# The last step of a one-layer vision tower written out by hand, with the last five tiles gated together

## The reference, cut to what matters

```
h = patches @ tok_W                                        # 768 -> 256
x = layernorm(h)
mod = gelu(x @ w1 + b1) @ w2 + b2                          # 256 -> 1024 -> 256
m = (x @ in_w + in_b) * mod
y = irfft(rfft(m over an image's 196 tokens) * rfft(taps))
h = h + y @ out_w + out_b
x = layernorm(h)
gate = softmax(x @ router_W.T + router_b)                  # 6 experts, the best 2 kept
h = h + x @ base_W.T + base_b + shared(x)
      + sum over experts of gate_e * (x @ A_e.T) @ B_e.T   # rank 16
```

## Time and profile before

| | us |
|---|---|
| median of 3 runs | 1297.09 (1296.03 to 1297.81) |
| the profiled execution, its own time | 1294.84 |
| span of its trace | 1293.0 |
| TensorE busy | 1239.2 (96%) |
| VectorE busy | 868.5 (67%) |
| ScalarE busy | 585.6 (45%) |
| GpSimd busy | 399.8 (31%) |

### The profile page before, as it was taken

The page is one execution under the profiler, slowest core; times in us unless marked ns, Lnnn a source line. Parts: engine busy times, 40 slices in busy tenths (PEclk is TensorE's granted clock), DMA queues, the critical chain, the costliest instruction groups (busy, mean ns, idle before and its releaser), DMA issues.

```text
span 1293.0 us, 21070 instructions
## 1 busy us (share of the span) xinstructions
PE 1239.2 (96%) x8148; PEld 1199.4 (93%) x8148; DVE 868.5 (67%) x2584; ACT 585.6 (45%) x1108; POOL 399.8 (31%) x462
## 2 busy tenths in 40 slices
PE   5999999999999999999999999999999999999964
PEld 5999999999999999999999999999999999999953
DVE  6467666667766666766666776666677666677575
ACT  6644544444444445454444444443545444444410
POOL 4532333232233333233323223332323332322100
PEclk9999999999999999999999999999999999999986
DMA  7111111101111110111110111111011111010000
GB/s 236 37 38 50 49 50 38 49 13 50 49 50 50 37 39 24 50 49 50 37 50 13 50 49 50 50 37 46 18 50 49 50 37 50 15 48 13 13 1 33
DMA packets 23182, 57.18 MB, mean 44 GB/s; under 512 B 2665, under 2 KB 18218, under 8 KB 19114
## 3 DMA queue, kind: packets, MB, share of 16 engines
q1 hardware_dynamic: 22266, 55.05, 12.2%
q10 hardware_dynamic: 816, 0.79, 0.2%
HBM read 42.98 MB, written 12.85 MB: 43 GB/s over the span
## 4 chain that ended last, share of the span: by engine, by line
PE 90%; DVE 5%; ACT 2%; issue 1%; POOL 1%; DMA 0%; POOLq 0%; DVEq 0%
PE rotating L953 16%; PE rotating L955 16%; PE rotating L954 16%; PE rows_ps L953 10%; PE rows_ps L954 10%; PE rows_ps L955 10%; PE turn L1095 5%; PE turn L1079 2%; ACT x_h L449 2%; DVE x_l L702 2%; PE turn L992 2%; PE turn L953 1%; PE turn L954 1%; PE turn L955 1%; PE rotating L1060 1%
## 5 line engine op out<-in xcount | busy, mean ns | idle before, releaser
L471 ACT ACTIVATE gelu<-rotating,biases 128x392 f32<-128x392 f32 x256 | 149.0, 583 | 203.6 <-PE rotating L955 203.4
L382 POOL TENSOR_TENSOR folded<-modulated 128x196 f32<-128x196 f32 x64 | 38.5, 601 | 588.1 <-DVE modulated L793 588.1
L369 POOL TENSOR_TENSOR gelu_l<-gelu,gelu_h 128x784 fp32r<-128x784 f32 x62 | 117.1, 1889 | 225.8 <-DVE norm L776 199.8
L354 POOL TENSOR_TENSOR patches_l<-patches,patches_h 128x384 fp32r<-128x384 f32 x186 | 184.4, 1020 | 0.2 <-ACT patches_h L429 0.2
L953 PE MATMUL rotating<-gelu_h,w_h 128*128 128x392 f32 x512 | 177.6, 347 | 0.0
L953 PE MATMUL rotating<-x_h,w_h 128*128 128x392 f32 x512 | 177.1, 346 | 0.0
L953 PE MATMUL rows_ps<-tokw_h,patches_h 128*128 128x256 f32 x576 | 167.8, 291 | 7.5 <-POOL patches_l L360 7.5
L955 PE MATMUL rotating<-x_h,w_l 128*128 128x392 f32 x512 | 174.6, 341 | 0.0
L954 PE MATMUL rotating<-x_l,w_h 128*128 128x392 f32 x512 | 174.5, 341 | 0.0
L955 PE MATMUL rotating<-gelu_h,w_l 128*128 128x392 f32 x512 | 174.0, 340 | 0.0
L954 PE MATMUL rotating<-gelu_l,w_h 128*128 128x392 f32 x512 | 173.9, 340 | 0.0
(11 more groups left out here) (203 smaller groups left out, 3007.2 us busy)
## 6 DMA issues: line engine op xcount, KB each, us to landing
patches<-dram_x_rest SPq DMA_DIRECT2D x31, 1152.0 KB, 5.1
out<-h_sb SPq DMA_DIRECT2D x32, 384.0 KB, 2.5
patches<-dram_x_first SPq DMA_DIRECT2D x3, 384.0 KB, 4.9
h_sb<-dram_x_second SPq DMA_DIRECT2D x1, 768.0 KB, 8.3
prod<-dram_tok_w ACTq DMA_DIRECT2D x2, 256.0 KB, 5.4
gelu<-dram_w SPq DMA_DIRECT2D x1, 512.0 KB, 6.4
norm<-dram_w SPq DMA_DIRECT2D x1, 384.0 KB, 6.1
gelu<-dram_w SPq DMA_DIRECT2D x1, 384.0 KB, 7.0
```

Source lines behind the costliest of these rows:

```text
L354: pool.tensor_tensor(patches_l[:, k, :], patches[:, k, :], patches_h[:, k, :].bitcast(F32), ALU.subtract).then_inc(pool_patches_lo, 1)
L369: pool.tensor_tensor(gelu_l[:, 2 * j:2 * j + 2, :], gelu[:, 2 * j:2 * j + 2, :], gelu_h[:, 2 * j:2 * j + 2, :].bitcast(F32), ALU.subtract)\
L471: act.activation(gelu[:, k, :], bank(g + 1, UP[k])[:, 0:GT], ACT.Gelu, bias=b1_bias[:, k:k + 1]).then_inc(act_gelu, 1)
```

## The change

The loop over i ends at 31. Step 32 and all that follows it stand in an order of their own, for each engine. In short, as against the order before (`last` is 31):

- In step 32 TensorE does the first two of eight parts of `mlp_down(31, 0)` ahead of `inverse_dft(30)` and the rest behind it, and `mixer_tiles(30)` stands after the first two parts of `mlp_down(31, 1)`. DVE does `gelu_lo(31, 2)` ahead of `spectrum_of_y(30)` and `finish(29)` after `gelu_lo(31, 3)`. `modulate(31, 0)` stands right after `y_lo(30)`, and `modulate(31, 1)` inside the chain of the layer norm (`meanwhile`). Before, both stood behind the chain and the normalisation.
- `turn_x2(30)` stands behind `turn_fold(31)`; `dft(31)` ahead of `base_route(30)`.
- `gate_exp(30)` moves from between `spectrum_of_y` and `whole_y` to after `normalise(31)`; `gate(30)` from there to after `x2_lo(32)`; `routed(30)` from ahead of `turn_x2(31)` to after the base products of the last tiles. Round 32 is normalised by ACT (`last_normalise`) while DVE does round 31.
- The five tiles of rounds 31 and 32 get one gate of 25 + 1 instructions. TensorE first makes only the 102 routing columns for all five (30 products, `last_routes_products`), and their 256 base columns later (30 products, `last_base_products`). The five tiles' scratch space and two constants, loaded by SP in step 31 ahead of the store of round 28, lie in the free buffer `patches`.
- The last output goes in three parts (two tiles, one, two), each added and stored once its products are done. POOL writes two rows of constants for it.

```diff
+LAST_TILES = 5
+LAST_PLACES = ((0, 0), (0, 1), (1, 0), (2, 0), (2, 1))
+LAST_BANKS = ((0, 1), (2,), (3, 4))
...
+        last_base = (rotating[:, 0], rotating[:, 1], turn[:, 0])
+        last_routes = turn[:, 1, 0:LAST_TILES * ROUTE_COLS].rearrange("p (t c) -> p t c", t=LAST_TILES)
+        last_gated_h, last_gated_l = y_h[0:ROUTED + 1, 0, :], y_l[0:ROUTED + 1, 0, :]
...
 @block.sync
-            for i in range(1, GROUPS + 1):
+            for i in range(1, GROUPS):
                 if i + 2 < ROUNDS:
                     load_patches(i + 2)
+                else:
+                    sp.wait_ge(pool_patches_lo, KT * (ROUNDS - 2))
+                    sp.dma_start(last_thr, last_rank_thr_d).then_inc(last_consts, 16)
+                    sp.dma_start(last_bias, last_router_bias_d).then_inc(last_consts, 16)
...
 @block.gpsimd
+            last = GROUPS - 1
+            pool.wait_ge(gate_done, last - 1)
+            gelu_lo(last, 0)
+            gelu_lo(last, 1)
+            fold(last, 0)
+            fold(last, 1)
+            pool.wait_ge(pe_out, 2 * last + 3)
+            pool.memset(y_h[ROUTED:ROUTED + 1, 0, :].bitcast(F32), 1.0).then_inc(last_ones_row, 1)
+            pool.memset(y_l[ROUTED:ROUTED + 1, 0, :].bitcast(F32), 0.0).then_inc(last_ones_row, 1)
...
 @block.scalar
+            y_sine(last - 1)
+            y_hi(last - 1)
             fold_hi(last)
+            x2_hi(last - 1, rows_ps, x2_h)
             y_sine(last)
             y_hi(last)
-            gated_hi(last - 1, turn[:, 0])
+            last_normalise()
             x2_hi(last, turn, x2_h)
             x2_hi(last + 1, rotating, x1_h)
-            gated_hi(last, rotating[:, 2])
-            gated_hi(last + 1, rotating[:, 2])
+            gated_hi(last - 1, rotating[:, 2])
+            last_gated_hi()
...
 @block.vector
+            fold_lo(last - 1)
+            gate_exp(last - 2, round_routes, round_room)
+            gate(last - 2, round_routes, round_room)
+            real_products(last - 1)
+            gated_lo(last - 2, bank(GROUPS, TURN_GATED))
+            imaginary_products(last - 1)
+            gelu_lo(last, 2)
+            spectrum_of_y(last - 1)
+            gelu_lo(last, 3)
+            finish(last - 2, rows_ps)
+            whole_y(last - 1)
+            y_lo(last - 1)
+            dve.wait_ge(dve_y_lo, DH * last)
+            modulate(last, 0)
+            add_mixer(last - 1, rows_ps[:, 2], bank(GROUPS, OUT)[:, 0:DIM])
+            stats = stats2(last - 1, 1)
+            layer_norm_scales(GROUPS + 1, stats, slice(1, 2), 3, meanwhile=lambda: modulate(last, 1))
+            normalise(last - 1, norm2, 1)
             fold_lo(last)
+            x2_lo(last - 1, rows_ps, x2_h, x2_l)
             real_products(last)
             imaginary_products(last)
             spectrum_of_y(last)
-            gate_exp(last - 1, rows_ps)
             whole_y(last)
             y_lo(last)
-            gate(last - 1, rows_ps)
             add_mixer(last, rotating[:, 1], rotating[:, 2, 0:DIM])
...
             normalise(last, norm2, 1)
-            dve.wait_ge(pe_turn_gated, last)
-            normalise(last + 1, norm1, 0)
-            gated_lo(last - 1, turn[:, 0])
-            finish(last - 1, rows_ps)
+            gate_exp(last - 1, round_routes, round_room)
             x2_lo(last, turn, x2_h, x2_l)
             x2_lo(last + 1, rotating, x1_h, x1_l)
-            gate_exp(last, rows_ps)
-            gate(last, rows_ps)
-            gated_lo(last, rotating[:, 2])
-            gate_exp(last + 1, turn)
-            finish(last, rows_ps)
-            gate(last + 1, turn)
-            gated_lo(last + 1, rotating[:, 2])
-            finish(last + 1, turn)
+            gate(last - 1, round_routes, round_room)
+            dve.wait_ge(last_consts, 32)
+            gate_exp(last, last_routes, last_room)
+            gated_lo(last - 1, rotating[:, 2])
+            gate(last, last_routes, last_room)
+            finish(last - 1, rows_ps)
+            last_gated_lo()
+            last_finish()
...
 @block.tensor
+            def last_routes_products():
+                pe.wait_ge(dve_x2_lo, DH * GROUPS + DH)
+                for t in range(LAST_TILES):
+                    hi, lo = (x2_h, x2_l) if t < 3 else (x1_h, x1_l)
+                    toks = slice(t % 3 * TILE, (t % 3 + 1) * TILE)
+                    for c in range(DH):
+                        ins = mm3(last_routes[:, t, :], hi[:, c, toks], lo[:, c, toks], wide_h[:, c, DIM:WIDE],
+                                  wide_l[:, c, DIM:WIDE], c == 0, c == DH - 1)
+                ins.then_inc(pe_route, 1)
...
+            mlp_up(last, 7)
+            pe.wait_ge(act_gelu, HC * last + 7)
+            mlp_down(last, 0, (0, 1))
+            inverse_dft(last - 1)
+            mlp_down(last, 0, range(2, HC))
+            pe.wait_ge(act_gelu, HC * last + 8)
+            mlp_down(last, 1, (0, 1))
+            pe.wait_ge(dve_result, last - 1)
+            pe.wait_ge(dve_y_lo, DH * last)
+            mixer_tiles(last - 1, rows_ps[:, 2], bank(GROUPS, OUT)[:, 0:DIM])
+            mlp_down(last, 1, range(2, HC))
             turn_fold(last)
+            turn_x2(last - 1, rows_ps, norm2)
+            dft(last)
             base_route(last - 1, rows_ps, x2_h, x2_l)
-            dft(last)
             inverse_dft(last)
             pe.wait_ge(dve_mod, DH * last + 2)
             pe.wait_ge(dve_y_lo, DH * last + DH)
             mixer_tiles(last, rotating[:, 1], rotating[:, 2, 0:DIM])
             mixer_tiles(last + 1, rotating[:, 0], None)
-            turn_gated(last - 1, turn[:, 0])
+            turn_x2(last, turn, norm2)
+            pe.wait_ge(act_last_norm, 1)
+            turn_x2(last + 1, rotating, norm1)
+            last_routes_products()
+            turn_gated(last - 1, rotating[:, 2])
+            last_base_products()
             routed(last - 1, rows_ps)
-            turn_x2(last, turn, norm2)
-            turn_x2(last + 1, rotating, norm1)
-            pe.wait_ge(dve_result, last)
-            base_route(last, rows_ps, x2_h, x2_l)
-            base_route(last + 1, turn, x1_h, x1_l)
-            turn_gated(last, rotating[:, 2])
-            routed(last, rows_ps)
-            turn_gated(last + 1, rotating[:, 2])
-            routed(last + 1, turn)
+            last_turn_gated()
+            last_routed()
```

More of the change, by code:

```diff
@@ L1 @@
+from collections import namedtuple
 from contextlib import ExitStack
@@ L332, in _ @@
                 weight(n)
-            for i in range(1, GROUPS + 1):
+            for i in range(1, GROUPS):
                 if i + 2 < ROUNDS:
                     load_patches(i + 2)
+                else:
+                    sp.wait_ge(pool_patches_lo, KT * (ROUNDS - 2))
+                    sp.dma_start(last_thr, last_rank_thr_d).then_inc(last_consts, 16)
+                    sp.dma_start(last_bias, last_router_bias_d).then_inc(last_consts, 16)
                 if in_range(i - 3):
                     store(i - 3)
-            for d in range(GROUPS - 2, ROUNDS):
-                store(d)
-            sp.wait_ge(result_out, 16 * ROUNDS)
+            last = GROUPS - 1
+            store(last - 2)
+            store(last - 1)
+            first = output_tiles(last)[0]
+            for n, tiles in enumerate(LAST_BANKS):
+                sp.wait_ge(dve_result, last + n + 1)
+                at, slot = first + tiles[0], (first + tiles[0]) % H_SLOTS
+                sp.dma_start(out_v[:, at:at + len(tiles), :], h_sb[:, slot:slot + len(tiles), :])\
+                    .then_inc(result_out, 16)
+            sp.wait_ge(result_out, 16 * (last + len(LAST_BANKS)))
         @block.gpsimd
@@ L707, in over_experts, with gate_exp @@
                 return a.rearrange("p (t a) -> p t a", a=1).broadcast_to([P, n, EXPERTS])
-            def gate_exp(d, rows):
-                n = len(output_tiles(d))
-                small = lambda c: gate_small[:, c, 0:n]
-                wide = lambda c: gate_wide[:, c, 0:n].rearrange("p t e -> p (t e)")
+            def gate_exp(e, routes, room):
+                n = room.n
+                small = lambda c: room.small[:, c]
+                wide = lambda c: room.wide[:, c].rearrange("p t e -> p (t e)")
                 done = [0]
@@ L739, in gate_exp, with gate @@
                 assert done[0] == EXP_STEPS
-            def gate(d, rows):
-                n = len(output_tiles(d))
-                small = lambda c: gate_small[:, c, 0:n]
-                wide = lambda c: gate_wide[:, c, 0:n].rearrange("p t e -> p (t e)")
+            def gate(e, routes, room):
+                n = room.n
+                small = lambda c: room.small[:, c]
+                wide = lambda c: room.wide[:, c].rearrange("p t e -> p (t e)")
                 done = [EXP_STEPS]
@@ L882, in _ @@
                 if in_range(tail):
-                    gate_exp(tail, rows_ps)
-                    gate(tail, rows_ps)
+                    gate_exp(tail, round_routes, round_room)
```

(27 more changed lines are left out.)

193 lines of the change are left out of this document (143 added, 50 removed).

## The result

| | before | after |
|---|---|---|
| median (6 runs each) | 1297.30 us (1296.03 to 1297.93) | 1288.11 us (1286.59 to 1289.22) |
| profiled execution, own time | 1294.84 | 1288.19 |
| span of its trace | 1293.0 | 1286.4 |

The ratio is 0.9933, 95% interval 0.9922 to 0.9944: the change makes the kernel 8.7 us faster by the ratio, 9.2 by the medians. The forecast was 1286.0 with a range of 1282.2 to 1289.8 and a gain of 11.1 us. The two profiles are only 6.6 us apart, since the profiled execution of before lay 2.5 us under its median and that of after on its own.

What follows compares the result with a forecast made beforehand. TensorE bounds the kernel for some 1200 us; from 1232 us one dependent chain across four engines does. Gains of 7.2 us up to the output projections and 3.9 behind them sum to 11.1: median 1286.0, range 1282.2 to 1289.8.

Steps and rivals of the forecast that it cites:

- rival (c): TensorE's clock falls early, between 1231 and 1236.4, or stays low in the narrow products: 1288.8 or 1289 us; chance 0.17.
- the clock is at half at 1242 to 1250: Sign named beforehand: half clock from inverse_dft(31) through the output projections would show the forecast wrong.
- terms one and two: Step 32 and the fold: inverse_dft(30)'s gap goes, 1.3 to 1.4 us; turn_fold(31) starts 3.5 us sooner, that included.
- term three: Fold to output projection: dft(31) result 0.4 us sooner, full clock giving 1.75 at inverse transform and 1.5 at projections.
- L: Moment of the first normalisation after the output projections: 1262.40 us before, forecast 1255.2.
- the first case of rival (c): Clock falls between 1231 and 1236.4; dft and base_route take twice as long, inverse transform 2.8 us later: 1288.8.
- a loss of "1.5 to 2.8": Microseconds lost if the clock still falls in the 2.5 us gap before the output projections.
- term four: Norm and operands: last operand ready at L + 5.7 instead of L + 7.6, gain 1.9 us.
- the unknown: Pace of 102-column products: 0.11 us taken, double at half clock; clock back after 5 us, all done by L + 11.4.
- the second case: Clock doesn't rise in the narrow run; base products and routed(30) end after the gate, holding last transposes 2 to 3 us: 1289.
- term five: One gate for five tiles: 6.4 us plus 0.5 for gated_lo(30), then 5.8 to the last addition at L + 24.2.
- rival (a): Clock never falls after the output projection: tail 1 us shorter, 14.5 us gained in all, 1282.6; chance 0.13.

Runs made afterwards that it cites:

- useless products everywhere: Changed kernel plus 256-column TensorE products that feed nothing, in waits up to the output projections, behind them and around the five-tile gate's transposes: 1281.66 us, ratio 0.9891.
- useless products up to the projections: Changed kernel plus 256-column products that feed nothing: 15 before turn_fold(31), 5 before dft(31), 18 after inverse_dft(31): 1285.14 us, ratio 0.9913.
- `modulate` late: Changed kernel with both modulate of group 31 put back behind the layer norm and its normalisation: 1292.57 us, ratio 0.9966.
- `gate_exp(30)` early: Changed kernel with gate_exp(30) between y_lo(31) and add_mixer(31), where DVE waits for TensorE, instead of behind normalise(31): 1286.89 us, ratio 0.9925.
- base products first: Changed kernel with the 30 base products ahead of the 30 routing products: 1290.94 us, ratio 0.9962.

## Why the prediction was right, and what it mis-sized

The time fell in the range, and the gaps that were to go went. But the clock took the course of rival (c), which had a chance of 0.17 and the times 1288.8 and 1289: the measured 1288.11 lies nearer to these than to the forecast of 1286.0, and the range holds because it was drawn to take (c) in. By a sign that the prediction named itself ("the clock is at half at 1242 to 1250") the forecast's course was wrong from 1248.9 on.

- **Step 32 and the fold** (terms one and two): right. `turn_fold(31)` came 3.7 us sooner, 3.5 forecast, with the play of 1 us between traces in it; undoing the two `modulate` costs 4.3 us. One step was right by luck: `gelu_lo(31, 2)` started 0.48 us sooner than worked out (1216.46) and took 0.48 longer (1.41, beside GpSimd), so the two sums ended at 1219.08 for 1219.1. And behind `modulate(31, 1)` come eight small instructions, not nine, with the same 2.43 us.
- **From fold to output projection** (term three): the order was right, two sizes were not. The clock fell at 1235.3, so `dft(31)` took 2.9 us instead of 1.6 and `base_route(30)`, meant to be hidden, held `inverse_dft(31)` for 0.2 us. It fell again at 1248.9 and the output projections took 5.3 us instead of 3.6. Only the inverse transform ran at full clock as forecast (1.93 us). The term was sized at 3.7 and measured 0.5: 1257.29 - 1253.07 = 4.2 for the first three terms, of which 3.7 belong to the first two. With useless products the stretch to L took 22.3 us for the forecast's 22.2, so at full clock the term is right, and what it had wrong is the clock. Both falls stood in the prediction, as the first case of rival (c) and as a loss of "1.5 to 2.8", and had too little weight.
- **Norm and operands** (term four): right, L + 5.4 against L + 5.7. That `gate_exp(30)` costs about 1 us there was seen too.
- **Narrow products**: the pace, the unknown, was right at both clocks. That the clock rises 5 us into their run was wrong. It stayed at half for all 6.4 us and rose only at 1272.8, 2.3 us into the base products; that cost 1.0 us, of which 0.3 came back by the operands, so the gate started 0.7 us later. Of the rival (c) the second case is thus what happened; the base products and `routed(30)` still ended before the gate (1276.4 and 1277.2), so its price of 2 to 3 us did not fall due.
- **The gate and the end** (term five): the gate took 6.9 us with `gated_lo(30)` in it, as forecast. The end took 6.6 instead of 5.8, at half clock from 1279.6 on.
- Sum in the profiles: 6.6 instead of 11.1, 4.5 us missing: 3.0 up to L, from term three, and 1.5 behind it (0.7 at the gate's start, 0.8 at the end). With useless products everywhere the kernel was 14.1 us (ratio) to 14.6 us (medians) under the kernel before, and rival (a), a clock that doesn't fall behind the output projection, had said 14.5.
- On the two rules of the Trainium skill (TensorE: Matmul & The Clock Gate). The formula of "LDWEIGHTS (loading the stationary operand)" has no clock in it, so by it the narrow products would take 107 ns at either; the runs show 113 ns at full and 215 ns at half. By "Part 4: PE-mode transpose" the clock should fall where TensorE has only transposes; of the four profiles in the table without useless products up to there it did in two (at 1235.3 and 1235.6) and not in the other two, which settles nothing.

Not tried: how many useless products would do, and a five-tile gate with wide products, for which PSUM has no room beside the transposed tiles.

## What to carry to other kernels

In a tail where one dependent chain crosses the engines, start each cross-engine hand-over (here a multiply that feeds another engine) before work that only its own engine needs: undoing that for two instructions cost 4.3 of the 8.7 us. Make first the columns that the chain waits for: undoing that cost 2.8 to 3.8. Put small instructions where their engine waits: that took 0.9 us off the wait for the narrow products' operands. Then price TensorE's part of such a tail at half clock unless something keeps it dense; where PSUM banks are free, products that nobody reads are a cheap way to do that, here 5.4 to 6.4 us of 1288. Splitting the last result took 0.9 us off the trace from the gate to the last addition; if it is split, let each store go as soon as its part is ready (another 1.0).

## What the runs showed of the hardware

- A product of 102 columns takes as long as one of 256 (0.113 and 0.115 us at full clock, 0.215 and 0.213 at half).
- TensorE can be busy all the time and the granted clock fall or stay low: 6.4 us of narrow products at half clock without a rise, in this and three more profiles that entered the run at half clock (useless products up to the projections, `modulate` late, `gate_exp(30)` early), and a fall at 1263.5 in the middle of such a run at full clock. With products of 256 columns it came back 1.7 to 4.7 us after they began (these four profiles, useless products everywhere, and base products first).
- Small DVE instructions with two inputs in SBUF took 0.59 and 0.56 us instead of 0.16 while GpSimd ran its fold, and the one between them, with one input, 0.17 (1231.58, 1232.29 and 1232.21 above). GpSimd's two instructions, and its own `gelu_lo` before them, stood at:

```profile
1215.15 1.89 POOL L421 TENSOR_TENSOR gelu_l<-gelu,gelu_h 128x784 fp32r<-128x784 f32 x1 [0.73 <-ACT gelu_h L538]
...
1231.56 0.60 POOL L434 TENSOR_TENSOR folded<-modulated 128x196 f32<-128x196 f32 x1 [5.07 <-DVE modulated L891]
...
1232.24 0.60 POOL L436 TENSOR_TENSOR folded<-modulated 128x196 f32<-128x196 f32 x1
```

Each of the two DVE instructions ends with GpSimd's, to 0.01 us. `gelu_lo(31, 2)`, which now starts while GpSimd's `gelu_lo` runs (until 1217.04), took 1.41 us instead of 0.93. The Trainium skill (SBUF — State Buffer, "SBUF: two separate sides") tells it as a lock: a DVE instruction with two SBUF inputs and a GpSimd instruction that reads SBUF share a pair of ports, and the one that starts first has it for its whole duration. The trace agrees. The two small instructions cost the norm's chain 0.8 us, off the path.
